# Counting the graph attention's edges with the operands of the counting matmul exchanged

## What is computed

```python
src = concatenate([edge_index[0], loops]); dst = concatenate([edge_index[1], loops])
e = leaky_relu(a_src[src] + a_dst[dst], 0.2)
e_max = segment_max(e, dst)
ee = exp(e - e_max[dst])
denom = segment_sum(ee, dst)
alpha = ee / (denom[dst] + 1e-16)
agg = segment_sum(h[src] * alpha, dst) + b_gat
```

## Time and profile before

| | us |
|---|---|
| median of 3 runs | 9333.57 |
| lowest and highest | 9332.01, 9335.05 |
| the profiled execution | 9331.56 |
| its span | 9329.9 |
| the loop over tiles and the counts after it, in the profile | about 3234 to 3527 |

### The profile page before, as it was taken

How to read it: one execution, slowest core, us unless ns; L and a number is a source line. 1 busy time by engine, 2 the same in 40 slices (tenths; PEclk the granted TensorE clock), 3 DMA queues, 4 the chain that set the end, 5 groups by cost and what they waited for, 6 DMA issues and landing times. The chain is left out here.

```text
span 9329.9 us, 128385 instructions
## 1 busy us (share of the span) xinstructions
PE 6463.7 (69%) x28206; PEld 4933.2 (53%) x28207; DVE 4563.9 (49%) x10633; ACT 3130.7 (34%) x7424; POOL 5764.7 (62%) x6163
## 2 busy tenths in 40 slices
PE   6749889988899897886899555554444454565552
PEld 3336666666666696775788344443333343344341
DVE  5547777777777656665677311111111141222225
ACT  3435666666666411111222133333333321111110
POOL 1136666666666304777772677777777767777762
PEclk9979999999999996776999777777776787777775
DMA  3256667776777533222666344443333341222115
GB/s 113 79 166 207 207 209 210 209 209 206 210 208 210 146 98 110 79 79 71 199 195 189 105 119 119 119 118 106 100 100 100 100 129 37 42 47 47 41 40 178
DMA packets 658024, 1226.09 MB, mean 131 GB/s; under 512 B 168236, under 2 KB 410080, under 8 KB 657747
## 3 DMA queue, kind: packets, MB, share of 16 engines
q0 software_dynamic: 296176, 717.44, 27.8%
q1 hardware_dynamic: 334117, 467.16, 15.9%
q10 hardware_dynamic: 27580, 39.79, 1.2%
HBM read 1087.91 MB, written 144.07 MB: 132 GB/s over the span
## 5 line engine op out<-in xcount | busy, mean ns | idle before, releaser
L955 POOL DMA_INDIRECT e_kv<-KV,e_idx x1712 | 1630.4, 952 | 765.1 <-issue 481.6
L2503 POOL DMA_INDIRECT s_x<-XN,s_idx x1712 | 1621.9, 947 | 589.5 <-issue 498.5
L2561 PE MATMUL s_psA<-s_x,s_oh 128*128 128x257 f32 x1712 | 661.5, 475 | 1121.0 <-DMA s_x<-XN,s_idx 1025.4
L2598 DVE TENSOR_TENSOR NS<-s_psA,NS 128x257 f32 x856 | 364.8, 426 | 1742.6 <-PE s_psA L2562 1742.4
L2922 POOL DMA_INDIRECT t_g<-G,t_idx x1024 | 1011.9, 988 | 311.3 <-issue 309.7
L1613 POOL DMA_INDIRECT SD<-o_pay,o_pos x880 | 925.5, 1052 | 317.6 <-issue 269.9
L2561 PEld LDWEIGHTS s_psA<-s_x,s_oh 128*128 128x128 f32 x1712 | 401.5, 242 | 1232.8 <-issue 1160.9
L1060 PE MATMUL e_psQ<-QA,e_oht 128*128 x3424 | 894.1, 407 | 199.8 <-issue 115.1
L1060 PEld LDWEIGHTS e_psQ<-QA,e_oht 128*128 128x128 f32 x3424 | 646.7, 199 | 367.5 <-issue 281.0
L3094 PE MATMUL t_psH<-t_xT,t_w 128*128 128x384 f32 (+1 forms) x1088 | 425.4, 558 | 355.7 <-ACT t_H L3072 335.2
L995 ACT ACTIVATE QA<-e_psA 128x264 f32 x856 | 332.0, 388 | 1000.6 <-PE e_psA L1080 990.8
(11 more groups left out here) (598 smaller groups left out, 11843.5 us busy)
## 6 DMA issues: line engine op xcount, KB each, us to landing
o_dbf<-DBF SPq DMA_DIRECT2D x128, 512.0 KB
f_w<-in_L_ffn_Wd_dram SPq DMA_DIRECT2D x57, 1024.0 KB
e_relb<-REL SPq DMA_DIRECT2D x107, 512.0 KB, 6.0
o_dlo<-DLO SPq DMA_DIRECT2D x128, 256.0 KB
e_kv<-KV,e_idx POOLq DMA_INDIRECT x1712, 3.8
s_x<-XN,s_idx POOLq DMA_INDIRECT x1712, 2.8
YD<-t_y ACTq DMA_DIRECT2D x50, 512.0 KB, 2.7
h_yt<-YD SPq DMA_DIRECT2D x10, 2560.0 KB, 17.7
```

The source lines that it names most:

```text
L955: pool.indirect_dma_start(kv[:, s, t, :], None, k.KV, bass.IndirectOffsetOnAxis(ap=idx[:, s, t:t + 1], axis=0)).then_inc(kv_in[s][g], 16)
L2503: pool.indirect_dma_start(x[:, s, t, 0:C], None, k.XN2, bass.IndirectOffsetOnAxis(ap=idx[:, s, t:t + 1], axis=0)).then_inc(x_in[s], 16)
L2561: pe.matmul(psA[:, u % 4, 0:C + 1], oh[:, o, 2 * u, :], x[:, s, 2 * u, :], start=True, stop=False)
```

## The change

The upper parts' one-hots become the weights (64 columns), the lower parts' the moving operand (128 columns); `psC` is then 64 x 128, transposed. At the end DVE copies `psC` into a new tile `turn`, PE transposes that into the first of the two PSUM tiles that the start had used, and DVE copies the result to `cnt2`. A new semaphore `kept` ties the three together.

```diff
-        self.psC = c.enter_context(nc.psum_tensor("c_psC", [P, HG], F32))
+        self.psC = c.enter_context(nc.psum_tensor("c_psC", [HG, P], F32))
+        self.turn = sb("turn", [HG, P])
@@ pe_start
-        pe.matmul(self.psC[:], k.zero1[:], k.ones[0:1, 0:HG], start=True, stop=True)
+        pe.matmul(self.psC[:], k.zero1[:, 0:HG], k.ones[0:1, :], start=True, stop=True)
@@ pe_step
-            last = pe.matmul(self.psC[:], self.oh_lo[:, s, :, j], self.oh_hi[:, s, :, j], start=False, stop=False,
+            last = pe.matmul(self.psC[:], self.oh_hi[:, s, :, j], self.oh_lo[:, s, :, j], start=False, stop=False,
                              skip_group_check=True)
+    def pe_end(self, pe):
+        pe.wait_ge(self.kept, 1)
+        pe.transpose(self.psT[0][:, 0:HG], self.turn[:], self.k.ident[0:HG, 0:HG]).then_inc(self.kept, 1)
@@ dve_end
         after(dve, self.counted, self.blocks - 1)
-        self.link(dve.tensor_copy(self.k.cnt2[:], self.psC[:]))
+        dve.tensor_copy(self.turn[:], self.psC[:]).then_inc(self.kept, 1)
+        dve.wait_ge(self.kept, 2)
+        self.link(dve.tensor_copy(self.k.cnt2[:], self.psT[0][:, 0:HG]))
@@ attention_output, tensor
             for b in range(NT, count.blocks):
                 count.pe_step(pe, b, b % 2)
+            count.pe_end(pe)
```

More of the change, by code:

```diff
@@ L1350, in __init__ @@
         self.psT = [c.enter_context(nc.psum_tensor(f"c_psT{i}", [P, TG], F32)) for i in range(2)]
-        self.psC = c.enter_context(nc.psum_tensor("c_psC", [P, HG], F32))
+        self.psC = c.enter_context(nc.psum_tensor("c_psC", [HG, P], F32))
+        self.turn = sb("turn", [HG, P])
         self.nat_in, self.setup, self.nat_done, self.turned, self.low_done, self.low_kept = (
             sem(n) for n in ("c_nat_in", "c_setup", "c_nat_done", "c_turned", "c_low_done", "c_low_kept"))
-        self.onehots, self.counted = sem("c_onehots"), sem("c_counted")
+        self.onehots, self.counted, self.kept = sem("c_onehots"), sem("c_counted"), sem("c_kept")
     def primed(self):
```

## The result

| | before | changed |
|---|---|---|
| median | 9332.79 us (6 runs, 9327.87 to 9335.05) | 9484.11 us (6 runs, 9483.77 to 9491.16) |
| span of the profiled execution | 9329.9 us | 9489.4 us |
| ratio to before | | 1.0166, 95% interval 1.0152 to 1.0179 |

The changed kernel is 151 us slower, and the interval lies well clear of 1. The forecast was 9484.

The account below looks back on a forecast made before the run. PE, without a gap in the loop, was taken as the bound. Counting matmuls 124 us, clock 25 and end 1 made 150; 9331.56 + 2.0 + 150 gave 9484 us, range 9440 to 9550.

Parts of the forecast that it names:

- step on the counting matmul: Counts on PE: stepped reading of the moving operand sets the 123 ns, 1.92 ns a column, so 246 after; chance 0.83.
- The matmuls in the loop: 50 blocks of 16 counts on PE, each matmul 0.123 us longer with no slack to take it: 98 us.
- a weight load that lies beside it: Counts on PE: loading 64 weight columns, at worst 123 ns and latency, is hidden beside a matmul of 246 ns.
- After the loop: Counting blocks behind the loop go from 2.06 to 3.94 us, covering DVE's 1.91: 14 x 1.88 = 26 us.
- The clock: PE's clock falls in some tiles towards the end of the longer counts, slowing transposes and projections: 25 us, bounds 0 and 80.
- a minority that pays part: In the loop, the clock falls in a minority of tiles, each paying part of at most 3.2 us.
- The 3.3 us: Counts running alone at the end before the clock is at 0.50, held against the changed block's 3.9 us.
- The end: At the stage's end, one more copy and pass in the hand-over, all on the path: about 1 us, bounds 0.5 and 1.5.
- the weights set the step: Rival for the counts: the weight load bounds the step, so 64 columns halve it to 62 ns; 9284 us, chance 0.06.
- both reads add up: Rival for the counts: weight and moving columns share one stock, step stays at 123 ns; 9334.6 us, chance 0.08.
- no overlap: Rival for the counts: load and matmul stop overlapping, step 369 ns; about 9665 us, chance 0.03.
- The estimate of 107 ns for a load of 128 columns: Skill's rule of weight columns at 1.2 GHz: 107 ns now, 53 after, a gain of 43 us in the loop (9292).

Follow-up runs that it names:

- weights_by_4: Kernel before, only the weights' one-hots (lower parts, 128 columns) laid out in groups of 4 edge columns; 9327.19 us, ratio 0.9995.
- moving_by_4: Kernel before, only the moving operand's one-hots (upper parts, 64 columns) laid out in groups of 4 edge columns; 9318.66 us, ratio 0.9986.
- swap_wide: Changed kernel, the weights' one-hots padded with 64 columns of zeros to 128; 9460.2 us, ratio 1.0138.
- early_only: Kernel before, only DVE's bias sum moved ahead of the one-hots; 9333.87 us, ratio 1.0.
- both_by_8: Kernel before, both one-hots laid out in groups of 8 edge columns, 16 bytes apart; 9333.53 us, ratio 1.0.
- wide_mid: swap_wide with 8 counts in the middle of their own tile's projection and 8 behind it; 11587.02 us on a slower chip, ratio 1.0118.
- swap_split: Changed kernel, each block cut in two: 8 counts behind the tile's projection, 8 ahead of the next one's; 9557.77 us, ratio 1.026.
- both2_early: Kernel before, both one-hots in groups of 2 edge columns and DVE's bias sum ahead of the one-hots; 9306.65 us, ratio 0.9973.
- swap_by_4: Changed kernel, both one-hots laid out in groups of 4 edge columns; 11452.82 us on a slower chip, ratio 1.0001.

## Why the prediction was right

Its step on the counting matmul carried it. It said that the reading of the moving operand sets the 0.123 us and argued from two rows, the matmul's record 112 ns above that of its packed like and the load's 49. `weights_by_4` and `moving_by_4` show just that, and `swap_wide` rules out the narrow weights. That the time came out to the microsecond is luck: the sum was 150 for 152, with errors of 12 and 17 us in its first term that largely cancel, and a term for the clock that was a guess.

1. *The matmuls in the loop*, 98 us forecast, 103.5 measured, from two errors that offset each other. The step was to grow by 0.123 us and grew within a block from 0.125 to 0.233: 800 x 0.108 = 86 us, 12 less. The price of a column falls a little with the width (with wide weights too, 0.240). And each block opens and closes more slowly with narrow weights: 2.07 - 16 x 0.108 = 0.34 us a tile, 17 us in 50, which the prediction had at nothing ("a weight load that lies beside it"). `swap_wide`, where the tile is 16 x 0.115 = 1.84 longer than before and nothing else, shows that it is the narrow weights.
2. *After the loop*, 26 us forecast, 23 measured, by the smaller step.
3. *The clock*, 25 us forecast, 25 measured (15 x 1.69). It was called the least certain term and was: the size came out right, but from other parts. More tiles were hit than "a minority that pays part" suggests (15 of 50, each with 1.69 of the 3.2 us). And the clock did not fall "towards the end of the counts": in the 15 long tiles it fell 4.3 to 4.8 us after the block's first matmul (3.8 in the first), behind the block's 3.9, among the transposes. The 3.3 us that the prediction measured by were one reading of a time that varies: from the start of the last tile's counts to the fall it is 3.3 us before, 3.4 in `early_only`, 3.9 in `weights_by_4` and 5.8 in `both_by_8`, with nearly the same counts. So a fall in some tiles was foreseen and its size was a guess that came true. What brings it on is shown in part, by `wide_mid`; `swap_split` shows that it is not enough to cut the counts in two.
4. *The end*, 1 us forecast, 0.7 measured.
5. The rivals: the weights set the step and both reads add up, out by `weights_by_4` and `swap_wide`; no overlap, out by the step of 0.233 with a load of 198 ns beside it. The estimate of 107 ns for a load of 128 columns, by which the first rival was priced a second time, doesn't hold here: `both2_early` loads 128 columns for each matmul at a step of 0.030 us.

The Trainium skill, page SBUF — State Buffer, section Door 1: The DMA port swizzle, was cited for lines of 16 bytes. The unit agrees with the table above. That bf16 may be stepped up to 8 elements at full bandwidth does not: at 8 elements (16 bytes) the price was full and at 4 (8 bytes) half, 0.96 ns against the 0.43 of rows 6, and the measurement decides. Nor do two hits in a line suffice here: 8 bytes give two, and it takes the four of 4 bytes to come near the packed rate.

## What to carry to other kernels

When a matmul takes longer than its columns explain, look for its like with packed operands elsewhere in the trace and compare matmul and load apart: the one that grew by nearly the whole step is the bound. For one-hots, put four edge columns side by side rather than sixteen: it costs DVE nothing here and halves what PE pays for reading them. And when a bound is removed, look at once for what was waiting just behind it; here it was a load whose issue hung on a sum that could as well stand earlier.

## What the runs showed that I had not expected

- The price of a moving bf16 operand is about 1.9 ns for each 16 bytes touched, with 8 to 32 bytes between columns; with 8 and with 32 bytes it is the same at both clock levels, and 32 bytes cost no more than 16. At 4 bytes the step follows the clock, 0.030 us at 1.00 and 0.053 at 0.50.
- Blocks with weights of 64 columns open later than with 128: the first load starts with its matmul, not 0.21 us ahead, some 0.33 us a block in all (0.23 net of the slightly shorter steps) and 0.38 for each cut. Zeros up to full width were worth 24 us in the changed kernel. Why the load doesn't run ahead is open.
- DVE writes a one-hot of 2048 bf16 in 1.21 us with 4 edge columns side by side, 1.23 with 8 or 16, and in 2.00 with 2.
- The lower clock struck at the same work more often when the counts were cut with only transposes between the halves (24 of 48 tiles) than uncut (14), and not at all with projections between them. In `swap_by_4` it didn't fall even with 14 blocks on end, where the same columns were read at half the price.
